# Macaron layer on one core: the outgoing tiles of the first mixture, and the routing of the second, moved into the attention loop

## Chip, cores, metric

One Trainium2 (trn2) chip, one NeuronCore. The metric is device time in microseconds of one launch, median of the runs. Engines: PE (TensorE), DVE (VectorE), ACT (ScalarE), POOL (GpSimd), and SP, which only issues DMAs here. Each engine runs its own instruction list in order; semaphores connect them.

## What is computed

The input has 2 x 2048 tokens of width 256, held in SBUF as 32 tiles of 128 tokens (`X`).

```python
x = x + 0.5 * ffn(layernorm(x))     # first mixture of experts
x = x + attn(layernorm(x))          # linear attention, 16 heads of 16
x = x + 0.5 * ffn(layernorm(x))     # second mixture, same weights
# ffn(h):  g = softmax(layer_norm(h) @ router_w.T); the two largest of 4 experts
#          hid = relu(layer_norm(h @ w1[e])) (512 wide); y_e = hid @ w2[e]
#          layer_norm(sum of the two y_e, weighted)
# attn:    Q, K, V projections; Z = cumsum over time of V K^T per head
#          Y_t = Q_t Z_t; out = Y @ Wo.T + bo
```

## The kernel before

The tokens of a mixture go in two groups G of 16 tiles (G = 0, 1 in the first mixture, 2, 3 in the second). **Routing** a group: normalise each tile (`quad_norm`, `quad_rstd`, `quad_factors`, four tiles a quad; `row` and `row_low` make an fp16 high and low part in `hrow`), transpose it (`row_T` on PE, copied by ACT), multiply by the router weights (`router`), choose experts for eight tiles, an octet (`logits`, `exps`, `choose`, `prefix`, `place`), and `scatter` each tile with two indirect DMAs from POOL's queue into the DRAM buffer `slots_in`, sorted by expert. `tables`, `positions` and `gates` then say which expert each block of 256 slots has and where each token's two results lie.

A **pair** is one block of 256 slots; a group has 19, a mixture 38. SP loads a pair (`load_slots`: two DMA transposes and one plain load, five pairs ahead), PE does `grams` (variances of the hidden layer), `layer1` and `layer2`, ACT and DVE the relu in two fp16 parts, POOL the standard deviations (`pair_std`), and SP stores the results in `slots_out` (`store_slots`). Routing group G + 1 runs beside the pairs of G, and the **outgoing tiles** of G beside the pairs of G + 1: POOL gathers a token tile's two results (`gather`, two indirect DMAs), ACT weights the first (`first_weighted`), DVE adds the second and takes statistics (`token_sum`), POOL the reciprocal root (`token_rstd`), DVE updates `X` (`token_out`). The outgoing tiles of the last group of a mixture have no pairs beside them: they run alone after the loop, and so does the routing of G = 2 (`route`), after attention.

**Attention** waits for all of X (`wait_ge(c_x, NT)` on every engine), does a prologue (POOL clears `qx`; scales, transposed weights, first block of Q, K, V), then 32 chunks of 128 tokens in blocks of four. Within a block's four chunks (t = 0 to 3) PE also does the next block's transposes, Q and K (t = 1) and V (t = 2). Per chunk: `scores` (four groups of heads), DVE masks them (`mask_scores`), ACT and POOL split them in a high part and a low part (`score_high`, `score_low`), PE `outputs` and `keys_values`, DVE `mask_kv`, POOL `add_state`, then PE `y_T` and `project` and DVE `update_x`. SP copies the queries apart by head for the scores (`expand`, eight DMAs per half block).

```python
    POOL, chunk c: score_low(c+1, 0..2); add_state(c)
    DVE,  chunk c: mask_scores(c+1, 0..1); update_x(c-1); mask_scores(c+1, 2..3); last_score_low(c+1); mask_kv(c)
    PE,   chunk c: scores(c+1), with y_T(c-1), project(c-1) between; outputs(c); keys_values(c)
```

## Time and profile before

| | us |
|---|---|
| median of 3 runs (1186.03 to 1187.82) | 1186.77 |
| the profiled execution | 1186.19 |
| its span, first to last instruction | 1184.3 |
| weights and routing of G = 0 | 0 to 118 |
| pairs of the first mixture | 118 to 392 |
| outgoing tiles of G = 1 | 392 to 454 |
| attention's prologue and its loop | 454 to 763 |
| routing of G = 2, alone | 763 to 844 |
| pairs of the second mixture | 844 to 1116 |
| outgoing tiles of G = 3, stores | 1116 to 1184 |

Busy over the span: PE 859.2 us (73%), DVE 773.1 (65%), POOL 634.1 (54%), ACT 528.3 (45%). The mean granted PE clock is 0.87 of full speed. The span is cut in stages that follow each other with little overlap, so shares of the whole say little: each stage is read by itself.

### The profile page before, as it was taken

What the parts mean: (1) busy time and instruction counts of PE and PEld (TensorE: products, weight loads), DVE (VectorE), ACT (ScalarE), POOL (GpSimd) and SP (SyncE); (2) the same over time, 40 slices, a digit from 0 to 9 for tenths busy, and PEclk for the clock granted to TensorE, in tenths of its full rate; (3) what the DMA queues carried; (4) which work ended last, traced back from release to release, by engine and by line L of the source; (5) the groups of instructions that cost most, each with busy time, mean ns of one, the idle gap of its engine ahead of it and who ended that gap; (6) DMA issues with size and microseconds to landing.
All of it is one profiled execution on the core that took longest, in us unless ns stands there. A gap on an engine that the chain in (4) does not pass through costs nothing.

```text
span 1184.3 us, 26374 instructions
## 1 busy us (share of the span) xinstructions
PE 859.2 (73%) x8346; PEld 677.6 (57%) x8346; DVE 773.1 (65%) x2160; ACT 528.3 (45%) x998; POOL 634.1 (54%) x707
## 2 busy tenths in 40 slices
PE   1543799989999202799999999730499989999600
PEld 1432688878888101466666666520388878888500
DVE  5567765776787366477777777643366675877355
ACT  2643466333434112467665666461266433444311
POOL 4154327533555476377778777537325462555275
PEclk9966899999999655899999999955599999999955
DMA  8052346656664320000000000003435655666332
GB/s 284 21 192 96 90 105 173 164 158 159 153 170 112 107 75 18 19 19 19 12 12 17 20 19 19 1 19 138 116 104 140 157 177 148 155 168 151 126 119 91
DMA packets 168026, 119.74 MB, mean 101 GB/s; under 512 B 95061, under 2 KB 158041, under 8 KB 167769
## 3 DMA queue, kind: packets, MB, share of 16 engines
q1 hardware_dynamic: 154626, 83.42, 26.7%
q0 software_dynamic: 12288, 33.57, 9.1%
q8 instruction: 77, 1.26, 0.5%
q10 hardware_dynamic: 984, 1.07, 0.3%
q14 instruction: 51, 0.42, 0.1%
HBM read 48.79 MB, written 45.09 MB: 79 GB/s over the span
## 4 chain that ended last, share of the span: by engine, by line
PE 54%; POOL 13%; DVE 11%; issue 10%; DMA 6%; ACT 5%; SPq 1%; ACTq 0%; POOLq 0%; DVEq 0%
POOL slots_in L503 6%; PE bank L1682 5%; PE bank L1669 5%; PE bank L1670 5%; PE bank L1671 5%; PE bank L1684 4%; PE bank L1683 4%; PE bank L1751 4%; PE bank L1752 4%; PE bank L1753 4%; DMA area<-slots_out,pos 4%; PE bank L1645 2%; PE bank L1851 2%; PE bank L1646 2%; PE bank L1532 2%
## 5 line engine op out<-in xcount | busy, mean ns | idle before, releaser
L511 POOL TENSOR_TENSOR stds<-vare,expo 128x4 f32<-128x4 f32 x76 | 80.4, 1058 | 200.0 <-DVE vare L794 196.5
L503 POOL DMA_INDIRECT slots_in<-area,spos x128 | 134.2, 1048 | 98.7 <-DVE spos L729 63.5
L1682 PE MATMUL bank<-w2h,area 128*128 x608 | 166.3, 274 | 3.2 <-DVE area L808 3.2
L1669 PE MATMUL bank<-area,w1h 128*128 128x256 f16 x608 | 168.2, 277 | 0.0
L1670 PE MATMUL bank<-area,w1h 128*128 128x256 f16 x608 | 168.2, 277 | 0.0
L1671 PE MATMUL bank<-area,w1l 128*128 128x256 f16 x608 | 168.0, 276 | 0.0
L1684 PE MATMUL bank<-w2h,area 128*128 x608 | 165.8, 273 | 0.0
L1683 PE MATMUL bank<-w2l,area 128*128 x608 | 165.8, 273 | 0.0
L527 POOL DMA_INDIRECT area<-slots_out,pos x128 | 126.0, 984 | 54.9 <-issue 30.5
L808 DVE SCALAR_TENSOR_TENSOR area<-bank,area 128x512 f16<-128x512 f32 x152 | 104.5, 688 | 76.6 <-ACT area L1271 74.1
L606 POOL TENSOR_TENSOR area<-area 128x512 f16<-128x512 f32 x96 | 119.3, 1265 | 56.1 <-ACT area L1452 56.1
L1271 ACT ACTIVATE area<-bank 128x512 f16<-128x512 f32 x152 | 90.0, 592 | 119.4 <-PE bank L1671 117.5
L1645 PE MATMUL bank<-gramh,area 128*128 x304 | 75.4, 284 | 55.6 <-DMA area<-slots_in 39.5
L1287 ACT ACTIVATE area<-area,gate 128x256 f32<-128x256 f32 x64 | 32.5, 508 | 177.2 <-DMA area<-slots_out,pos 177.2
L1279 ACT ACTIVATE area<-bank,stds 128x256 f32<-128x256 f32 x152 | 71.4, 470 | 80.3 <-PE bank L1684 80.1
L1753 PE MATMUL bank<-area 128*128 128x16 f16 (+2 forms) x704 | 101.9, 213 | 0.0
L1751 PE MATMUL bank<-area 128*128 128x16 f16 (+2 forms) x704 | 99.3, 213 | 2.4 <-POOL area L606 1.4
L1752 PE MATMUL bank<-area 128*128 128x16 f16 (+2 forms) x704 | 100.9, 212 | 0.0
L1452 ACT ACTIVATE area<-area 128x512 f16<-128x512 f32 x128 | 78.2, 627 | 43.1 <-DVE area L1157 42.4
L1157 DVE SCALAR_TENSOR_TENSOR area<-bank,causal 128x512 f32<-128x512 f32 x128 | 84.8, 685 | 16.8 <-POOL area L606 9.7
L1646 PE MATMUL bank<-graml,area 128*128 x304 | 75.4, 285 | 0.0
L780 DVE SCALAR_TENSOR_TENSOR area<-area 128x512 f32<-128x512 f16 x76 | 51.9, 683 | 35.3 <-DMA area<-slots_in 35.0
(267 smaller groups left out, 2231.4 us busy)
## 6 DMA issues: line engine op xcount, KB each, us to landing
area<-slots_in SPq DMA_DIRECT2D x76, 256.0 KB, 3.1
slots_out<-area SPq DMA_DIRECT2D x152, 128.0 KB, 3.2
X<-in_L_attn_x_dram SPq DMA_DIRECT2D x8, 512.0 KB, 8.7
slots_in<-zrow SPq DMA_DIRECT2D x16, 256.0 KB, 2.4
area<-area SPq DMA_DIRECT2D x128, 32.0 KB, 2.0
out_dram<-X SPq DMA_DIRECT2D x32, 128.0 KB, 1.8
area<-slots_in SPq DMA_TRANSPOSE x152
area<-in_L_ffn_w_dram SPq DMA_DIRECT2D x4, 512.0 KB, 11.1
```

The lines of the kernel that those rows point to most:

```text
L503: pool.indirect_dma_start(slots_in[G % 2], bass.IndirectOffsetOnAxis(spos[:, O % 2, k, j:j + 1], 0), hrow[:, t].rearrange("p c d -> p (c d ...
L527: pool.indirect_dma_start(d[:, i % R_C], None, slots_out[G % 2], bass.IndirectOffsetOnAxis(pos[:, G % 2, k, t:t + 1], 0)).then_inc(g_y[i % ...
L606: pool.tensor_tensor(shl[:, c % 2, 1, g], sm[:, g], shl[:, c % 2, 0, g], ALU.subtract).then_inc(a_sl, 1)
L1669: pe.matmul(o, w1h[c][m][:, bass.ds(e, 1), :], a[:, c], start=(c == 0), stop=False)
L1670: pe.matmul(o, w1h[c][m][:, bass.ds(e, 1), :], a[:, KC + c], start=False, stop=False)
L1671: last = pe.matmul(o, w1l[c][m][:, bass.ds(e, 1), :], a[:, c], start=False, stop=(c == KC - 1))
L1682: pe.matmul(o, Rh[:, p % 2, k, rows], w2h[k][:, bass.ds(e, 1), :], start=(k == 0), stop=False)
L1683: pe.matmul(o, Rh[:, p % 2, k, rows], w2l[k][:, bass.ds(e, 1), :], start=False, stop=False)
L1684: last = pe.matmul(o, Rl[:, p % 2, k, rows], w2h[k][:, bass.ds(e, 1), :], start=False, stop=(k == HC - 1))
L1751: pe.matmul(o, lh, rh, start=start, stop=False, **kw)
L1752: pe.matmul(o, lh, rl, start=False, stop=False, **kw)
L1753: return pe.matmul(o, ll, rh, start=False, stop=stop, **kw)
```

## The change

Everything that lay between the last pair of the first mixture and attention's loop, and between that loop and the first pair of the second, is put elsewhere:

- The outgoing tiles of G = 1 go in chunks 0 to 17 of attention: chunk c gathers tile c, weights and sums tile c - 1, and updates X with tile c - 2. They use buffers of their own (`yA1`, `yB1`, `acc1`).
- The routing of G = 2 goes in chunks 5 to 28: one row per chunk from chunk 7 on, octets chosen from chunks 16 and 24, four scatters in each of chunks 19 to 22 and 27 to 30. Its rows are transposed by DMA (`turn_row`, on SP) and no longer by PE and ACT.
- The rows of G = 2 need 32 KB per partition while attention holds its own buffers. They take the place of the second weights: `w2h` and `w2l` become one tile `w2all`, written to DRAM (`w2_kept`, 2 MB) when the first mixture begins and read back after SP's first five pair loads of the second.
- Attention's prologue goes beside the first mixture's pairs (`ahead`): weights loaded at the start, maxima at j = 14, scales at 16, transposed weights from 16, POOL's clearing of `qx` at j = 0 of the second group, the first rows at 10 to 13, the first queries ahead of the last `layer2`.
- The queries of attention are expanded per chunk (`expand(c)`, eight DMAs of half the size for each of 32 chunks, not for each of 16 halves), and `hTh`, `hTl` and `qx` have other shapes.

```diff
+    w2_kept = nc.dram_tensor("w2_kept", (P, 2 * HC * E * D), F16).ap()
...
-            def expand(n):
-                wait(sp, a_qp, n + 1)
-                for part in range(2):
-                    cols = slice(part * BT // 2, (part + 1) * BT // 2)
-                    wait(sp, a_s, NG * TB * (n - 1) + NG * 2 * (part + 1))
-                    for j in range(HPC):
-                        rows = slice(j * HD, (j + 1) * HD)
-                        sp.dma_start(qx[rows, j, :, :, cols], qp[rows, :, :, cols]).then_inc(a_qx[part], 16)
+            def expand(c):
+                wait(sp, a_qp, c // TB + 1)
+                wait(sp, a_s, NG * (c - 1))
+                cols = slice(c % TB * P, (c % TB + 1) * P)
+                for j in range(HPC):
+                    rows = slice(j * HD, (j + 1) * HD)
+                    sp.dma_start(qx[rows, c % 2, j], qp[rows, :, :, cols]).then_inc(a_qx[c % 2], 16)
+            def turn_row(i):
+                sp.wait_ge(r_hl, i + 1)
+                wait(sp, r_L, i - 1)
+                sp.dma_start_transpose(turned_of(i), rows_of(i).rearrange("p c d -> p (c d)")
+                                       ).then_inc(l_tT[i % 2], 16)
+            def attention():
+                sp.wait_ge(a_zero, 1)
+                expand(0)
+                expand(1)
+                for c in range(NT):
+                    if c + 2 < NT:
+                        expand(c + 2)
+                    if row_in(c) is not None:
+                        turn_row(row_in(c))
...
+                else:
+                    sp.wait_ge(m_w2, 16)
+                    sp.dma_start(w2flat, w2_kept).then_inc(m_w2, 16)
...
             def attention():                        # POOL
-                pool.wait_ge(c_x, NT)
...
                         add_state(c)
+                        if c < GT:
+                            gather(GT + c)
+                        if 1 <= c <= GT:
+                            token_rstd(GT + c - 1)
+                        if quad_in(c) is not None:
+                            quad_rstd(quad_in(c))
+                        if quad_in(c - 1) is not None:
+                            quad_again(quad_in(c - 1))
+                        for i in moves_in(c):
+                            scatter(i)
...
                             mask_scores(c + 1, 1)   # DVE
+                        if 2 <= c <= GT + 1:
+                            token_out(GT + c - 2)
                         if c > 0:
+                            wait(dve, a_wo, c)
+                            if octet_in(c, 0) is not None:
+                                logits(octet_in(c, 0))
+                            if octet_in(c, 2) is not None:
+                                place(octet_in(c, 2))
                             update_x(c - 1)
...
+                        if 1 <= c <= GT:
+                            token_sum(GT + c - 1)
+                        if row_in(c) is not None:
+                            row_low(row_in(c))
+                        if quad_in(c) is not None:
+                            quad_norm(quad_in(c))
+                        if octet_in(c, 1) is not None:
+                            choose(octet_in(c, 1))
...
+                        if 1 <= c <= GT:            # ACT
+                            first_weighted(GT + c - 1)
+                        if row_in(c) is not None:
+                            row(row_in(c))
...
-                    route(G)                        # PE, second mixture
+                    pe.wait_ge(a_x, NT)
```

How it moves the lists. POOL inside attention's loop, from the start of a block to the third chunk (L606 and L703 are `score_low`, L612 and L709 `add_state`, L596 and L693 `add_bias`). Before:

```order
L606 TENSOR_TENSOR area<-area 128x512 x3
L612 TENSOR_TENSOR area<-area 128x256
L606 TENSOR_TENSOR area<-area 128x512 x3
L596 TENSOR_TENSOR X<-X,boB 128x1024
L612 TENSOR_TENSOR area<-area 128x256
L606 TENSOR_TENSOR area<-area 128x512
```

And now, for one of the blocks of chunks 4 to 15:

```order
L703 TENSOR_TENSOR area<-area 128x512 x3
L709 TENSOR_TENSOR area<-area 128x256
L610 DMA area<-slots_out,pos 128x256 x2
L600 TENSOR_TENSOR ars<-ave,nhalf 128x1
L703 TENSOR_TENSOR area<-area 128x512 x3
L693 TENSOR_TENSOR X<-X,boB 128x1024
L709 TENSOR_TENSOR area<-area 128x256
L610 DMA area<-slots_out,pos 128x256 x2
L600 TENSOR_TENSOR ars<-ave,nhalf 128x1
L569 TENSOR_TENSOR xrs<-xve,nhalf 128x4
L703 TENSOR_TENSOR area<-area 128x512
```

Each chunk has two gathers (L610) and a reciprocal root (L600) behind its `add_state`, and two chunks of a block one more root of the routing (L569, L574).

DVE inside the loop, from the second chunk of a block (t = 1) to the third. Before, from the end of the chunk (L1127 is `query_low`, L1157 `mask_scores`, L1170 `update_x`):

```order
L1175 SCALAR_TENSOR_TENSOR area<-bank,sameh 128x256
L1127 TENSOR_TENSOR area<-area 128x2x512
L1157 SCALAR_TENSOR_TENSOR area<-bank,causal 128x512 x2
L1170 TENSOR_TENSOR X<-bank,X 128x256
L1157 SCALAR_TENSOR_TENSOR area<-bank,causal 128x512 x2
```

Now (L1242 is `query_low`, L1272 `mask_scores`, L1285 `update_x`):

```order
L1242 TENSOR_TENSOR area<-area 128x2x512
L926 SCALAR_TENSOR_TENSOR area<-area,gate 128x256
L929 BN_STATS ast<-area 128x6
L931 BN_AGGR amv<-ast 128x2
L932 TENSOR_SCALAR ave<-amv 128x1
L777 TENSOR_TENSOR w2all<-area,w2all 128x256
L758 BN_STATS xst<-X 128x6 x4
L761 BN_AGGR xmv<-xst 128x2 x4
L763 TENSOR_SCALAR xve<-xmv 128x4
L1272 SCALAR_TENSOR_TENSOR area<-bank,causal 128x512 x2
L937 SCALAR_TENSOR_TENSOR area<-area,amv,ong 128x256
L941 SCALAR_TENSOR_TENSOR X<-area,ars,X 128x256
```

Between `query_low` and the next chunk's masks stand `token_sum` (L926 to L932), `row_low` (L777) and `quad_norm` (L758 to L763), and `token_out` (L937, L941) stands between the second and the third mask.

SP in the first mixture, behind the fifth pair load. Now:

```order
L458 DMA area<-slots_in 128x2x512
L478 DMA area<-in_L_attn_Wq_dram 128x2x256
L478 DMA area<-in_L_attn_Wk_dram 128x2x256
L478 DMA area<-in_L_attn_Wv_dram 128x2x256
L478 DMA area<-in_L_attn_Wo_dram 128x2x256
L481 DMA w_kept<-w2all 128x8192
L452 TENSOR_LOAD rtab
```

The weights' loads (1 MB) and the copy of `w2all` (2 MB) stand ahead of the sixth pair's load; before, L435 loaded the weights after the last store.

## Rows read from the trace of the kernel before

**Rows 1.** Stages: stretch, length, busy PE, PEld, DVE, ACT, POOL; clock, DMA share, GB/s.

```profile
393.00:454.00 61.00, 0.00 (x0) 0.00 (x0) 33.34 (x95) 8.12 (x16) 41.59 (x48) 0.53 0.30 88
454.00:494.00 40.00, 23.03 (x99) 13.46 (x100) 19.61 (x38) 13.75 (x21) 15.11 (x17) 0.66 0.05 13
494.00:762.00 268.00, 253.02 (x2862) 175.85 (x2861) 197.51 (x305) 169.93 (x296) 199.31 (x226) 0.99 0.07 16
762.00:847.00 85.00, 18.02 (x202) 14.02 (x201) 32.97 (x152) 24.55 (x51) 42.13 (x42) 0.52 0.22 78
```

**Rows 2.** Timeline of PE, around the last layer2 and attention's second chunk.

```profile
391.86 0.27 PE L1684 MATMUL bank<-w2h,area 128*128 x1
...
493.13 0.39 PE L1751 MATMUL bank<-area 128*128 128x512 f16 x1 [0.52 <-DVE area L1157]
493.35 0.38 PE L1752 MATMUL bank<-area 128*128 128x512 f16 x1
```

**Rows 3.** PE: eight f32 transposes; its wait at the first group's end; SP's expand DMAs.

```profile
610.23 1.04 PE L1737 MATMUL bank<-identf,h 128*128 128x128 f32 x8
...
PE bank L1645 <- DMA area<-slots_in: 2.2, 1, 2.2
...
L429 SPq DMA_DIRECT2D area<-area x128: 585/595/1571, 482.3 to 733.7; - x128
```

**Rows 4.** The chain of waits in attention's prologue: maxima, and the scales' first and last step.

```profile
456.15 2.05 DVE mx L1099 x3
...
462.40 0.17 DVE mxa L846
...
464.69 0.27 DVE bvB L1115
```

**Rows 5.** One block of attention by chunk (t = 0 to 3), columns as in Rows 1.

```profile
601.20:608.00 6.80, 6.08 (x77) 4.09 (x77) 5.17 (x12) 4.26 (x9) 5.66 (x15) 1.00 0.01 4
608.00:620.20 12.20, 12.20 (x109) 7.61 (x110) 7.70 (x12) 9.44 (x16) 9.36 (x8) 1.00 0.01 2
620.20:629.40 9.20, 9.20 (x109) 7.32 (x108) 6.92 (x12) 5.02 (x10) 6.62 (x5) 1.00 0.20 48
629.40:636.00 6.60, 5.65 (x76) 3.91 (x76) 6.11 (x8) 3.77 (x7) 4.42 (x4) 1.00 0.07 16
```

**Rows 6.** Groups by line: gathers (393 to 454), scatters and `row_low` (762 to 847).

```profile
L527 POOL DMA_INDIRECT area<-slots_out,pos x32 | 31.1, 972 | 18.7 <-DMA slots_out<-area 11.0 <-issue 7.7
...
L503 POOL DMA_INDIRECT slots_in<-area,spos x32 | 31.9, 997 | 25.6 <-DVE spos L729 16.2 <-issue 9.4
...
L675 DVE TENSOR_TENSOR area<-h,area 128x256 f16<-128x256 f32 x16 | 6.6, 423 | 14.3 <-ACT area L1247 14.3
```

**Rows 7.** Two DVE lines and one of POOL: ns shortest/median/longest, first and last start.

```profile
L1164 DVE TENSOR_TENSOR area<-area x32: 691/1140/1643, 495.6 to 755.8; 128x512 f16<-128x512 f32 x32
...
L1133 DVE TENSOR_TENSOR area<-bank,area x16: 678/686/692, 484.1 to 729.3; 128x512 f16<-128x512 f32 x16
...
L606 POOL TENSOR_TENSOR area<-area x96: 1147/1157/2146, 493.8 to 755.2; 128x512 f16<-128x512 f32 x96
```

**Rows 8.** From attention's end to the second mixture's first layer2: chain, then timelines.

```profile
763.26 1.41 DVE xst L655 x4
...
832.68 0.96 POOL L503 DMA_INDIRECT slots_in<-area,spos  x1 [0.30 <-issue]
...
854.65 0.53 SPq L396 DMA_DIRECT2D area<-slots_in  x1
...
859.66 0.27 PE L1682 MATMUL bank<-w2h,area 128*128 x1
```

**Rows 9.** Four loads of 256 KB on SP's queue: timeline, then the last one's landing.

```profile
393.09 0.39 SPq L435 DMA_DIRECT2D area<-in_L_attn_Wq_dram  x1
...
394.58 0.47 SPq L435 DMA_DIRECT2D area<-in_L_attn_Wo_dram  x1
...
area<-in_L_attn_Wo_dram SPq DMA_DIRECT2D x1, 256.0 KB, 4.3
```

More of the change, by code:

```diff
@@ L285, in macaron_kernel @@
             "kv_added"))
-        a_qx = [sem(f"a_q_expanded{half}") for half in range(2)]
+        a_qx = [sem(f"a_q_expanded{b}") for b in range(2)]
+        l_tT = [sem(f"rows_T_{b}") for b in range(2)]
+        m_w2 = sem("w2_kept_and_back")
         dve_done = sem("dve_done")
@@ L344, in token_bank, with octet_in, row_in, router_in @@
             return bank[3] if i < GT else bank[4]
+        ROW_AT = 7
+        LOGITS_IN = [ROW_AT + 2 + TO * (o + 1) - 1 for o in range(GO)]
+        def octet_in(c, d):
+            return GO * 2 + LOGITS_IN.index(c - d) if c - d in LOGITS_IN else None
+        def row_in(c):
+            return 2 * GT + c - ROW_AT if 0 <= c - ROW_AT < GT else None
+        def router_in(c):
+            return row_in(c - 2)
+        def moves_in(c):
+            for o, at in enumerate(LOGITS_IN):
+                if at + 3 <= c < at + 3 + TO // 2:
+                    t = 2 * GT + TO * o + 2 * (c - at - 3)
+                    return t, t + 1
+            return ()
+        def quad_in(c):
+            return 2 * GQ + (c - 5) // TB if c % TB == 1 and 0 <= (c - 5) // TB < GQ else None
         @block.sync
@@ L1392, in mixture, with ahead, queries_ahead @@
                         row_T(i0 + GT + t)
+                    if f == 0:
+                        ahead(g - G, j)
+                if f == 0:
+                    queries_ahead()
                 for k in range(2):
                     scale_out(p0 + NP - 1, k)
-                for t in range(GT):
-                    first_weighted(i0 + GT + t)
+                if f == 1:
+                    for t in range(GT):
+                        first_weighted(i0 + GT + t)
+            def ahead(second, j):
+                if not second and j in (17, 18):
+                    weight_high(j - 17)
+                if second and j in (0, 1):
+                    weight_high(2 + j)
+                if second and j in (10, 11):
+                    h_rows(0, range(2 * (j - 10), 2 * (j - 9)))
+                if second and j == 12:
+                    hT_high(0)
+            def queries_ahead():
+                for o in range(GO):
+                    act.wait_ge(sc_h[o], 32 * TO * 2)
+                qk_copy(0, 0, qf[:, 0])
+                query_high(0)
             def h_rows(n, tiles):
@@ L1429, in query_high @@
             def query_high(n):
-                for part in range(2):
-                    wait(act, a_qx[part], NX * n)
+                for b in range(2):
+                    wait(act, a_qx[b], NX * 2 * n)
                 wait(act, a_qf, 4 * n + 2)
@@ L1549, in row_T @@
                 pe.wait_ge(r_hl, i + 1)
-                wait(pe, r_hT, i)
+                wait(pe, r_hT, turned(i))
                 if i == 0:
@@ L1728, in mixture, with ahead @@
                         row_T(i1 + t)
+                    if f == 0:
+                        ahead(g - G, j)
+                if f == 0:
+                    queries_keys(0, 0)
                 for k in range(2):
                     layer2(p0 + NP - 1, k, e[p0 + NP - 1])
+            def ahead(second, j):
+                if not second and j == 14:
+                    maxima_T(3)
+                if not second and j == 15:
+                    maxima_all(3)
+                if not second and j in (16, 17, 18):
+                    weight_T(j - 16)
+                if second and j == 0:
+                    weight_T(3)
+                if second and j == 11:
+                    pe.wait_ge(a_wl, 3)
+                    pe.wait_ge(a_wh, 4)
+                    rows_out_T(0)
             def rows_out_T(n):
```

285 lines of the change are left out of this document (161 added, 124 removed).

## The prediction

> **What bounds the kernel now.** I read the windows by stage first. Two stretches leave PE nearly idle: the outgoing tiles and the prologue (393 to 494, PE busy 23 of 101 us), and the routing (762 to 847, PE 18 of 85) [rows 1]. In the 268 us of attention's loop PE is busy 253, so the loop is PE's; but POOL has 199 and DVE 198 there, so each has only some 70 us free. The idle stretches are bought with that room. Then I read one block of the loop by chunk: 34.8 us, of which POOL works 26.1 and DVE 25.9; PE fills the chunks t = 1 and t = 2 wholly, while in t = 0 and t = 3 DVE has 1.6 and 0.5 us free and POOL 1.1 and 2.2 [rows 5]. So new work in t = 0 and t = 3 lengthens the loop at once.
>
> The sum is made against the profiled execution, 1186.2 us (span 1184.3, 1.9 around it); the median lies 0.6 above it.
>
> **A, the prologue's work beside the pairs: +12.** PE gets 24 f32 transposes at 1.04 / 8 = 0.13 us [rows 3], 3.1 us, and 12 matmuls of 512 columns at 0.22 us, the distance of two neighbours [rows 2], 2.6 us. PE is full in these pairs, so all 5.7 count. It also waits in order for others: for DVE's maxima 2.05 us, for the scales from 462.40 to 464.96, 2.6 us [rows 4], and for ACT's first rows some 1.7. That is 6.3, less the 2.2 us that PE waits for the second group's slots anyway [rows 3], since the maxima and scales fall just before that: +4. The weights and the 2 MB copy stand ahead of the sixth pair's load on SP; five pairs are loaded by then and cover them, so 0 to 5 us, I take 2. POOL's clearing (one 7 us instruction) falls where it has no gather; cover gone, it would delay one pair by under 5. A is 6 to 20.
>
> **B, what stood between: -87.8.** From the last `layer2` (ends 392.13) to the scores of chunk 1 (493.13) are 101.0 us [rows 2]. What is left: 12 matmuls for the keys (2.6 us), eight transposes (1.0), 24 matmuls of 256 columns for the values (at half of 0.22, 2.6), twelve for chunk 0's scores (2.6) and the copies between, some 11 us in sequence; and SP, after its last two stores (about 1.6 us), issues 16 expand DMAs at 0.595 each [rows 3], 9.5, and 2 to land: 13.2. SP is the later: 101.0 - 13.2 = 87.8, between 80 and 90.
>
> **C, attention's loop: +80.** Step by step.
> POOL: 16 outgoing tiles cost what the tail cost, 41.6 us [rows 1], plus 0.3 of issue time for each of 32 gathers [rows 6]: 51, or 3.2 per chunk. Routing costs 42.1 + 9.4 = 51.5 in the same way [rows 1, 6], of which scatters are four per chunk in eight chunks, 5.1 us each time. Together 102 against 69 free: **at least +33**, even if POOL never waits.
> DVE: the tail's 33.3 us are 2.1 per tile [rows 1]; the routing's 33.0 [rows 1] are 0.42 per row [rows 6], per quad 1.4 of statistics [rows 8] and some small steps, about 2.7 with them, and the rest, some 15, for the two octets and the tables. Together 66 against 70 free.
> DVE is also slower beside POOL: its subtraction with both inputs in SBUF (L1164) has a median of 1140 ns, and the same shape with one input in PSUM (L1133) 686 [rows 7]. The 0.45 us between them I add to each of the new two-input steps (three per tile, one per row).
> By block, then: block 0 (chunks 0 to 3), no routing yet, +6. Blocks 2 and 3: DVE 25.9 + 4 x 2.1 + 4 x 0.4 + 2.7 + 16 x 0.45 = 45.8, so +11, and 1 for waits: +12 each; POOL 26.1 + 12.8 + 2.0 = 40.9 is close behind. Block 1, with one row, +10. Block 4 (last tile, quad, first octet, first scatters) +9. Block 5: POOL 26.1 + 15.3 = 41.4, +8, since chunk t = 1 takes one set of scatters free. Block 6 (octet, tables) +9. Block 7: POOL 13.8 of 22.4 us and 15.3 more: +9 with its waits. Sum 75, and 5 for the longer round between engines, since `token_out` waits for POOL between two masks and holds the scores behind it. C is 33 at the least; I take 60 to 105 as its own range.
> Hidden: ACT gets 8.1 us (tiles) and less than 24.6 (routing, whose copies of transposed rows are gone) into 98 free. PE had 18 us for the routing at a clock of 0.52 of full speed, transposes included [rows 1]; without them and at full clock under 8 are left, where PE now waits longer than that. SP gets 128 more DMAs at 0.6 us, 4.8 per chunk in all, and 16 transposes; a chunk is 6.6 at the shortest, so its queue keeps up, unless `turn_row`, which waits for DVE's row and stands ahead of the next `expand`, makes it late; that is a rival.
>
> **D, routing taken out: -70.** Before, attention ended at 763.2 and the last scatter's issue at 833.64 [rows 8]. Now the last scatter is issued in chunk 30, within a microsecond of attention's end, and from there the second mixture starts as before: 70.4, less 0.5.
>
> **E, the second weights come late: +7.** SP issued the fifth pair's last load at 855.2, 21.5 us after the last scatter [rows 8]; the 2 MB are behind it. 1 MB took from 393.09 to 394.58 + 4.3 = 398.9, 5.8 us [rows 9], so 2 MB take 11.6: landed at 866.8 on the old scale, and `layer2` was at 859.66 [rows 8]. 0 to 15. What is late next is nothing: the sixth pair's slots land two pairs before use.
>
> Sum: 12 - 87.8 + 80 - 70 + 7 = -58.8, so **1127 us**, faster by 5%. The end of the kernel (68 us) is untouched.
>
> **A rule weighed.** The row first: L606 on POOL, which also reads SBUF, has a median of 1157 ns and a longest of 2146, DVE's L1164 of 691 to 1643 [rows 7]: they do hold each other up. The Trainium skill, "SBUF — State Buffer", section "Who interferes with whom", says that a DVE instruction with two SBUF inputs and a GpSimd instruction that reads SBUF exclude each other, and that the later one waits for the whole of the other. By that, this change puts more of both kinds side by side. The trace agrees for DVE's median; for POOL only the longest shows it. By the rule in full the loop would be the third rival; by the rows it is the 0.45 us above.
>
> **Rivals.**
> *POOL's floor.* The engines shift against each other by up to a chunk, waits vanish and C falls to 33 to 60, say 45: 1092 us. For it: POOL's 69 free us would then be used whole. Against: PE's t = 1 chunk holds everybody for 12.2 us, and DVE is nearly as full as POOL.
> *The round is longer.* `expand` waits behind `turn_row`, which waits for ACT's row, behind ACT's wait for the gather. In 16 chunks SP then issues 1.2 + 4.8 + 2 us late into a 6.6 us chunk: about 1.5 us each, 24; with some 10 more of waits C is 105 to 135: at 115, 1162 us. For it: SP's list is in order. Against: there is a chunk of slack.
> *Slower: DVE and POOL lock each other.* Each of the 96 L606 takes its longest, 2146 for 1157 ns [rows 7], +0.99 us: 95 us more on the engine that sets the pace, so C is 175 and the time 1222. It decides from C = 139 on, that is 1.8 us per chunk above my sum. Against: only a few of the 96 are long today, with DVE 74% busy.
> That the parts do not overlap is no rival: the lists above show them within the loop. Were the weights' return much slower (27 us), it is 15 us and inside the range.
>
> **Numbers.** My forecast (1108 to 1153) 0.61; POOL's floor (1080 to 1108) 0.20; longer round (1153 to 1186) 0.15; lock 0.04. Leaving out a tenth on each side, the range is 1093 to 1162. A difference under 0.2% (2.4 us) could not be told from none. Faster 0.96, same 0.01, slower 0.03.
>
> **What would show it.** Chunk 1's scores 10 to 15 us after the last `layer2`; blocks 2 and 3 of the loop at 44 to 49 us with POOL and DVE busy over 85%, PE under 75%; the loop as a whole 340 to 360 us; PE waiting 5 to 10 us for the DMA of `w2all` at the second mixture's first `layer2`. I am wrong if a block stays under 41 or goes over 52 us, or if PE waits in the first mixture for more than 12 us above before.

## The result, and the profile after

| | before | after |
|---|---|---|
| median, us (5 runs each, side by side) | 1186.95 | 1192.67 |
| span of the profiled execution | 1184.3 | 1191.8 |

The ratio is 1.0032, 95% interval 1.0017 to 1.0048: **slower by 0.3%**, where 1127 us was forecast. I cut the profiled execution as the prediction did. The windows by stage (columns as in [rows 1]) of the changed kernel, then the one stage of the kernel before that [rows 1] lacks, then its loop and the changed one from the first `update_x` to the last:

```profile
118.00:417.71 299.71, 272.48 (x2490) 226.87 (x2491) 211.42 (x670) 134.27 (x269) 133.61 (x141) 0.95 0.55 140
417.71:430.30 12.59, 9.07 (x58) 5.28 (x55) 5.46 (x8) 5.30 (x8) 2.12 (x1) 1.00 0.15 42
430.30:836.00 405.70, 304.51 (x2982) 198.39 (x2982) 309.18 (x545) 192.28 (x347) 279.49 (x314) 0.86 0.15 39
836.00:864.90 28.90, 13.61 (x100) 9.20 (x100) 17.50 (x73) 7.28 (x14) 6.76 (x7) 0.72 0.70 172
442.00:835.60 393.60, 295.06 (x2899) 192.85 (x2897) 300.11 (x528) 184.47 (x332) 269.25 (x297) 0.86 0.15 40
```

```profile
118.00:392.13 274.13, 261.08 (x2450) 219.79 (x2450) 193.99 (x640) 126.17 (x255) 124.84 (x126) 0.97 0.55 140
505.00:762.90 257.90, 245.38 (x2785) 171.11 (x2783) 189.53 (x291) 162.76 (x282) 189.24 (x209) 1.00 0.07 16
```

The terms, by the same boundaries (end of the last `layer2`, first scores of chunk 1, end of attention, first `layer2` of the second mixture):

| term | forecast | measured, us |
|---|---|---|
| A, prologue beside the pairs | +12 | 417.71 - 392.13 = +25.6 |
| B, what stood between | -87.8 | 12.6 - 101.0 = -88.4 |
| C, attention's loop | +80 | 405.7 - 270.1 = **+135.6** |
| D and E, routing out, weights late | -63 | 29.1 - 96.4 = -67.3 |
| after that | 0 | +2.1 |

They add up to 7.6, and the spans differ by 7.5. The idle stretches went about as forecast (156 us, 151 forecast); the loop and the first mixture took 161 back.

These are terms of one execution. The first mixture is the same code in the changed kernel and in twelve of the kernels below (e1 to e7, e9 to e11, e14, e16), and its last `layer2` begins between 408.92 us (e6) and 417.44 (the changed kernel, the latest of all), with a median of 413.3. So A is +17 to +26, and about +21 is the usual value.

No engine is full in the loop: of 393.6 us DVE is busy 300, PE 295, POOL 269. Windows of four chunks, from `update_x` to `update_x`; the prediction had blocks 2 and 3, which the third of them and the next (54.6 us) lie over, at 44 to 49 us:

```profile
442.00:497.40 55.40, 41.84 (x433) 27.94 (x431) 44.94 (x65) 24.78 (x44) 42.18 (x48) 0.88 0.13 35
497.40:552.90 55.50, 41.47 (x374) 26.67 (x374) 42.74 (x80) 26.00 (x47) 38.49 (x44) 0.82 0.13 34
552.90:610.80 57.90, 41.50 (x392) 26.42 (x392) 43.48 (x83) 28.02 (x51) 38.96 (x44) 0.84 0.16 37
```

All of these windows are above 52 us, which the prediction had named as a sign of being wrong. DVE's 43 us of work in a block are near what the prediction's sum gives (45.8); it expected them to fill the block, and they fill 75 to 81% of it. PE's waits in the loop (waiting line, releaser, sum, times, longest), and SP's longest:

```profile
PE bank L1930 <- DMA area<-area: 24.0, 8, 4.7
PE bank L1930 <- DVE area L1248: 21.4, 8, 4.0
PE bank L1930 <- DVE X L1285: 17.3, 10, 4.5
PE bank L1930 <- DVE hTl L1205: 8.4, 4, 2.6
...
SPq L507 <- DVE w2all L777: 118.4, 16, 16.6
```

L1930 is the first line of the helper that makes most of PE's products; L1248 is `ktok_low`, L1285 `update_x`, L1205 the low part of the transposed rows, L507 `turn_row`. Before, PE stood idle for 15 us in the whole loop (268.0 - 253.0). And DVE's lines there, with the mean of one in ns: L1279, `last_score_low` (L1164 in [rows 7], mean 1154), L941, the last step of `token_out` (485 where it ran alone), and L773, a step of `quad_factors` (170 there):

```profile
L1279 DVE TENSOR_TENSOR area<-area 128x512 f16<-128x512 f32 x32 | 53.8, 1682 | 7.7 <-ACT area L1605 7.7
L941 DVE SCALAR_TENSOR_TENSOR X<-area,ars,X 128x256 f32<-128x256 f32 x16 | 23.9, 1495 | 7.7 <-issue 6.7 <-DVE area L937 0.5
...
L773 DVE TENSOR_SCALAR r2t<-r2t 128x4 f32<-128x4 f32 x4 | 3.2, 802 | 0.1
```

One case, as the timelines of DVE and POOL show it (start, duration):

```profile
574.39 1.07 DVE L770 SCALAR_TENSOR_TENSOR xnr<-xmv,xrs 128x4 f32<-128x4 f32 x1
575.38 0.15 DVE L772 TENSOR_TENSOR r2t<-r2t,xrs 128x4 f32<-128x4 f32 x1
575.57 1.01 DVE L773 TENSOR_SCALAR r2t<-r2t 128x4 f32<-128x4 f32 x1
576.49 1.28 DVE L1248 TENSOR_TENSOR area<-bank,area 128x512 f16<-128x512 f32 x2
...
574.30 2.26 POOL L703 TENSOR_TENSOR area<-area 128x512 f16<-128x512 f32 x2
```

Two of `quad_factors`' steps of 128x4 end, within 0.1 us, with POOL's two subtractions; they stand ahead of `ktok_low` in DVE's list, and PE waits for that one, 3.98 us, until 577.23. A DVE step can be held by several POOL instructions in a row, too. Here `last_score_low`, 0.68 us at its shortest, takes 6.21, and ends 0.55 us after the fourth POOL instruction that had followed without a gap:

```profile
445.60 6.21 DVE L1279 TENSOR_TENSOR area<-area 128x512 f16<-128x512 f32 x1
...
445.58 3.37 POOL L703 TENSOR_TENSOR area<-area 128x512 f16<-128x512 f32 x3
448.92 2.34 POOL L693 TENSOR_TENSOR X<-X,boB 128x1024 f32<-128x1024 f32 x1
```

Two theories follow. **The round**: a step added ahead of what PE waits for lengthens each chunk, whatever share of DVE is free. **The lock**: DVE is held by POOL, more than I had priced, wherever the step stands.

### The profile page after: what moved, and what is told of

It is laid out like the page before. It is cut to its first block and busy times, and to the rows that moved or that the text cites. A ratio compares the mean times of both kernels' runs of the same rounds, so it can differ in the third digit from the quotient of the medians.

```text
span 1191.8 us, 26435 instructions
## 1 busy us (share of the span) xinstructions
PE 895.7 (75%) x8282; PEld 688.3 (58%) x8282; DVE 824.3 (69%) x2172; ACT 514.9 (43%) x982; POOL 629.9 (53%) x707
## 5 line engine op out<-in xcount | busy, mean ns | idle before, releaser
L1845 PE MATMUL bank<-w2all,area 128*128 x608 | 166.6, 274 | 7.0 <-DMA w2all<-w_kept 4.8
L1846 PE MATMUL bank<-w2all,area 128*128 x608 | 166.3, 274 | 0.0
L1847 PE MATMUL bank<-w2all,area 128*128 x608 | 166.3, 273 | 0.0
L610 POOL DMA_INDIRECT area<-slots_out,pos x128 | 126.3, 987 | 45.9 <-issue 29.4
L586 POOL DMA_INDIRECT slots_in<-area,spos x96 | 103.9, 1082 | 74.2 <-DVE spos L831 48.5
L703 POOL TENSOR_TENSOR area<-area 128x512 f16<-128x512 f32 x96 | 118.3, 1253 | 46.6 <-ACT area L1605 46.5
L1930 PE MATMUL bank<-area 128*128 128x16 f16 (+2 forms) x704 | 107.5, 221 | 43.3 <-DMA area<-area 24.0
L1932 PE MATMUL bank<-area 128*128 128x16 f16 (+2 forms) x704 | 107.8, 220 | 0.0
L1931 PE MATMUL bank<-area 128*128 128x16 f16 (+2 forms) x704 | 107.5, 220 | 0.0
L1806 PE MATMUL bank<-gramh,area 128*128 x304 | 77.3, 289 | 30.6 <-DMA area<-slots_in 12.1
L1930 PEld LDWEIGHTS bank<-area 128*128 128x128 f16 x704 | 60.0, 99 | 53.8 <-DMA area<-area 25.7
L1272 DVE SCALAR_TENSOR_TENSOR area<-bank,causal 128x512 f32<-128x512 f32 x128 | 82.5, 681 | 10.7 <-PE bank L1932 8.0
## 6 DMA issues: line engine op xcount, KB each, us to landing
area<-in_L_ffn_w_dram SPq DMA_DIRECT2D x4, 512.0 KB, 12.8
```

Of the source, the lines that this page charges most:

```text
L586: pool.indirect_dma_start(slots_in[G % 2], bass.IndirectOffsetOnAxis(spos[:, O % 2, k, j:j + 1], 0), rows_of(i).rearrange("p c d -> p (c d ...
L610: pool.indirect_dma_start(d[:, i % R_C], None, slots_out[G % 2], bass.IndirectOffsetOnAxis(pos[:, G % 2, k, t:t + 1], 0)).then_inc(g_y[i % ...
L703: pool.tensor_tensor(shl[:, c % 2, 1, g], sm[:, g], shl[:, c % 2, 0, g], ALU.subtract).then_inc(a_sl, 1)
L1845: pe.matmul(o, Rh[:, p % 2, k, rows], w2h[k][:, bass.ds(e, 1), :], start=(k == 0), stop=False)
L1846: pe.matmul(o, Rh[:, p % 2, k, rows], w2l[k][:, bass.ds(e, 1), :], start=False, stop=False)
L1847: last = pe.matmul(o, Rl[:, p % 2, k, rows], w2h[k][:, bass.ds(e, 1), :], start=False, stop=(k == HC - 1))
```

## Experiments

Ratios are to the kernel before, run beside each. "Loop" is from the first `update_x` to the last, in one profiled execution: 257.9 us before, 393.6 changed. What a kernel gains over the changed one is given by medians. By the ratios it is 1 to 3 us less: 6 (e1), 25 (e5), 13 (e6), 40 (e7), 20 (e14), 10 (e16). The loop alone, free of the first mixture's variation, gives 5, 18, 13, 38, 17 and 10.

### Which part costs: e1 to e4

e1 moves the transposing DMA behind the next expanding ones:

```diff
-                    if row_in(c) is not None:
-                        turn_row(row_in(c))
+                    if row_in(c - 1) is not None:
+                        turn_row(row_in(c - 1))
```

> The change with one edit: SP issues the DMA transpose of a routing row one chunk later, behind the next chunk's eight expand DMAs and not ahead of them. Theory 'round' (the loop is long because its steps follow each other across engines, and SP's turn_row, which waits for DVE's row_low at the end of a chunk, holds the expand DMAs that PE's scores need): PE's wait for the expand DMAs in the loop falls from 24 us to under 5 and the kernel is 15 to 35 us faster, near 1165. Theory 'lock' (DVE and POOL hold each other up and the length is theirs): the wait moves to another name and the time stays within 5 us of 1192.

Measured: 1183.53 us, ratio 0.9981 (0.9959 to 1.0004), 9 us under the changed kernel (6 by the ratios), loop 388.7. That is neither theory's time. PE's wait for the DMA fell from 24.0 us to 1.4, as the round theory said, but waits for ACT and DVE rose in its place, as the lock theory said.

e2 runs the outgoing tiles of G = 1 alone, after the first mixture, and leaves the routing in the loop; e3 does the reverse; e4 leaves both out of the loop, so that only the early prologue, the weights in DRAM and the queries expanded per chunk are new. The calls leave the loop and come back, unchanged, outside it, as in e2:

```diff
-                        if c < GT:
-                            gather(GT + c)
-                        if 1 <= c <= GT:
-                            token_rstd(GT + c - 1)
...
-                if f == 1:
+                if True:
                     for t in range(GT + 1):
```

> The change with the outgoing tiles taken out of attention's chunks and run alone behind the first mixture, as before; the routing stays beside attention. The tail comes back with 58 us. Theory 'lock': the tiles bring 48 of the two-input DVE steps and 32 gathers, so most of the loop's growth of 149 us goes with them, over 90, and the kernel is near 1155. Theory 'round' with SP as its centre: chunks 7 to 22 keep their long round through turn_row, the loop loses only 50 to 60 and the kernel is near 1190 to 1200.

> The change with the routing of G = 2 taken out of attention's chunks and run alone behind it (rows still turned by DMA), the outgoing tiles stay beside attention. Routing alone comes back with 60 to 75 us. Theory 'round': chunks 7 to 31 get most of their length back, the loop loses 80 to 100, kernel near 1165 to 1180. Theory 'lock': the loop loses 45 to 60, since the tiles' steps stay, kernel near 1205.

> The change with both taken out of attention: what is left of it is the prologue beside the pairs, the weights kept in DRAM and the expand per chunk. Both theories: the loop is back at 270 to 280 us, so the kernel is near 1186 - 40 (prologue) + 15 (its work beside the pairs) + 7 (weights) = 1160 to 1175. If it is over 1185, the expand per chunk or the prologue's part costs what the loop seemed to cost.

| | us | ratio, interval | loop |
|---|---|---|---|
| e2, routing in the loop | 1205.27 | 1.0175, 1.0137 to 1.0214 | 349.2 (+91.3) |
| e3, tiles in the loop | 1189.81 | 1.0044, 1.0024 to 1.0063 | 324.9 (+67.0) |
| e4, neither | 1190.71 | 1.0047, 1.0027 to 1.0067 | 257.9 (0) |

e4's loop is as long as before (257.9 us, PE busy 245.38 in both): 256 smaller DMAs cost the loop nothing. Tiles alone cost 67 and routing alone 91, together 136: the two costs overlap. No theory had the times of e2 and e3: e2's loop lost 44 us (over 90 or 50 to 60 were expected), e3's 69 (80 to 100 or 45 to 60). e4, expected at 1160 to 1175, came to 1190.71, and by its stages the early prologue is why: the first mixture is 23.0 us longer (15 expected), from there to the first `update_x` it is only 24.5 shorter (88.4 for 112.9; 40 expected), and what follows the loop is 7.5 longer (7 expected). In e3, tile steps stretch a block (492.0 to 543.0) from 34.8 us to 51, with DVE busy 37.6 of it, POOL 36.1 and PE 39.3.

### Place in the queue: e5 to e7

e5 moves `token_out` from ahead of `update_x`, between the masks, to the chunk's end. e6 leaves only the reads out of PSUM of `logits` and `place` there, and moves the rest and `quad_factors` to the end. e7 does both, and e1's move. No step is removed.

```diff
-                        if 2 <= c <= GT + 1:
-                            token_out(GT + c - 2)
                         if c > 0:
...
+                        if 2 <= c <= GT + 1:
+                            token_out(GT + c - 2)
                         if 1 <= c <= GT:
                             token_sum(GT + c - 1)
+                        if octet_in(c, 0) is not None:
+                            logits_rest(octet_in(c, 0))
...
+                        if quad_in(c - 1) is not None:
+                            quad_factors(quad_in(c - 1))
```

> The changed kernel, with the outgoing step (token_out) moved on VectorE from ahead of update_x to the end of the chunk, just before token_sum; nothing is removed. The round theory (what stands ahead of update_x lengthens each chunk, since TensorE waits for update_x and its transposes): the 1.5 us mean of 16 such steps and their place beside the gathers leave the round; the loop from first to last update_x comes down from 393.6 us by 16 x 1.5 to 2.4 = 24 to 38 us, and the time to 1155 to 1170. The lock theory (VectorE is held by GpSimd's two-operand instructions wherever the step stands): the step costs the same at its new place and the queue behind it moves on as late; the loop changes by less than 8 us, the time stays at 1184 to 1196, and the mean of the step stays near 1.5 us.

> The changed kernel, with the routing's small steps moved on VectorE to the end of the chunk: of logits and place only the read out of PSUM stays ahead of update_x, and quad_factors no longer stands ahead of ktok_low. Round theory: in the chunks that hold them the 4 to 8 us between the masks and ktok_low go down; loop shorter by 15 to 30 us, time 1160 to 1178. Lock theory: each of these small steps is held for 1 to 2 us wherever it stands, so the loop changes by less than 8 us and the time stays at 1184 to 1196.

> Both moves of the two runs before, and the transposing DMA of the routing rows one chunk later, behind the next expanding DMAs. Round theory: the gains add up to 45 to 75 us: 1117 to 1148 us, and the loop 320 to 350 us. Lock theory: the gain is that of the late DMA alone (about 9 us): 1176 to 1186 us.

| | us | ratio, interval | loop |
|---|---|---|---|
| e5 | 1166.58 | 0.9821, 0.9800 to 0.9843 | 375.3 |
| e6 | 1177.31 | 0.9924, 0.9908 to 0.9941 | 380.8 |
| e7 | 1150.36 | 0.9696, 0.9672 to 0.9719 | 355.7 |

The same work in another order is 42 us faster, and the parts nearly add up: 26 (e5), 15 (e6) and 9 (e1) against 42; in the loop 18, 13 and 5 against 38. That is the round in each of the three, not the lock theory's less than 8 us (about 9 in e7), though the loops gained less than expected (18 for 24 to 38, 13 for 15 to 30, 38 for 44 to 74) and e7 came 2 us above its range. e5's lines show that the lock is not apart from it:

```profile
L1279 DVE TENSOR_TENSOR area<-area 128x512 f16<-128x512 f32 x32 | 56.6, 1768 | 7.7 <-ACT area L1605 7.7
...
L941 DVE SCALAR_TENSOR_TENSOR X<-area,ars,X 128x256 f32<-128x256 f32 x16 | 11.4, 711 | 0.6
```

At its new place `token_out`'s step is held far less (711 ns, not 1495; one at 548.23 us, beside two gathers of POOL, takes 0.48 us); `last_score_low`, which did not move, is held as before. In e7 the loop is

```profile
437.50:793.20 355.70, 289.42 (x2899) 191.66 (x2896) 287.53 (x528) 185.41 (x332) 271.58 (x297) 0.88 0.17 44
```

with its first block at 45.4 us, DVE busy 42.1 of them: there DVE comes near to setting the pace, as the prediction had it.

### The first mixture: e8

```diff
-                if not second and j == 14:
+                if not second and j == 12:
                     attention_maxima()
-                if not second and j == 15:
+                if not second and j == 14:
                     max_row(3)
-                if not second and j == 16:
+                if not second and j == 15:
                     attention_scales()
```

(and TensorE's two steps one pair earlier, the first rows' turn one pair later.)

> The kernel of e7_all_late, with the prologue's steps beside the first mixture's pairs spaced out: on VectorE the maxima of the attention weights two pairs earlier, their row and the scales one pair earlier; on TensorE their two steps one pair earlier; the turn of the first block's rows (TensorE, ScalarE, VectorE) one pair later. Theory: term A came to 25.6 us and not 12 because TensorE stood 5.4, 4.7 and 2.7 us for exactly these three steps, placed in the same pair as the step that feeds them. Then these 12.8 us go, and the time is 1137 to 1145 against 1150. Rival: the stretch is longer because VectorE has too much to do there; then the waits come back at other lines and the time stays at 1148 to 1153.

In the changed kernel PE's waits of the first mixture are these (the fourth and fifth of them are the turn of the first rows and the first weight):

```profile
PE bank L1806 <- DVE var L891: 8.6, 2, 8.1
PE bank L1699 <- DVE mx L1212: 5.4, 1, 5.4
PE bank L1806 <- issue: 4.9, 9, 1.2
PE bank L1914 <- ACT h L1553: 4.7, 1, 4.7
PE bank L1924 <- DVE bvB L1230: 2.7, 1, 2.7
```

Measured: 1140.69 us, ratio 0.9607 (0.9591 to 0.9624), 9.7 below e7, with those three waits gone and the one for `mxd` grown from 0.7 to 3.3 us. The theory holds: a step and the one that feeds it stood in one pair.

### Three ways to mend the loop further: e9, e11, e13

e9 gives `last_score_low` to POOL. e11 moves the prefix matmul, `place` and the scatters one chunk later, and leaves out the loop's `positions(2)` and `gates(2)`. e13 (on e12, below) puts `mask_kv` ahead of `last_score_low`. Of e9's edit, the line that changes engine:

```diff
-                dve.tensor_tensor(shl[:, c % 2, 1, NG - 1], sm[:, NG - 1], shl[:, c % 2, 0, NG - 1],
+                pool.tensor_tensor(shl[:, c % 2, 1, NG - 1], sm[:, NG - 1], shl[:, c % 2, 0, NG - 1],
```

> The kernel of e7_all_late, with the low part of the fourth score group (last_score_low) on GpSimd instead of VectorE: VectorE loses 32 steps, 66.0 us of busy time, GpSimd gains 32 of about 1.2 us = 38 us. Lock theory (VectorE's busy time is in good part time in which it is held by GpSimd, and it sets the block): VectorE falls from 42 to 34 us of a block of 49, and the loop gets 10 to 30 us shorter: 1120 to 1140. Floor theory (GpSimd, at 39 of 49 us, is as near to its own end as VectorE): GpSimd comes to 44 us a block, PE waits for its low parts instead, and the loop is unchanged or up to 15 us longer: 1150 to 1165.

> The kernel of e7_all_late, with the prefix matmul, place and the scatters one chunk later (so that TensorE does not stand for choose, 5.7 us in two waits), and without the loop's positions(2) and gates(2), which the second mixture computes again. Theory: 5.7 us of TensorE's wait and about 3 us of VectorE in chunk 28 leave: 1141 to 1147. Rival: VectorE sets the chunk wherever the wait shows, and only the left-out steps count: 1147 to 1151.

> The kernel of e12_steps_before_query, with mask_kv ahead of last_score_low in each chunk. Theory: TensorE's projection waited 10.4 us for mask_kv, which stood behind a step that GpSimd holds for 1 to 4 us; that wait goes and the time falls by a further 5 to 12 us. Rival: mask_kv has to wait for TensorE's keys_values, and last_score_low behind it gets late for the next outputs: no gain, or up to 8 us slower.

Measured: e9 1157.28 us (ratio 0.9751, 0.9705 to 0.9796), e11 1151.31 (0.9706, 0.9687 to 0.9725), e13 1143.64 (0.9632, 0.9594 to 0.9670). None gains in time. In e9 DVE's busy time falls by 41 us, to 246.0 in this window, and the loop grows by 7, to 363.1:

```profile
437.50:800.00 362.50, 287.57 (x2899) 189.50 (x2898) 246.00 (x498) 185.69 (x333) 303.10 (x328) 0.87 0.17 43
```

POOL's busy time grew by 32 us, `query_low` went from a mean of 1319 to 2578 ns, PE waits 12.1 us for POOL (as the floor theory said, whose range the time is in) and 17.6 us for `update_x` (5.6 in e7). In e11 the loop is 5.6 us shorter than e7's (350.1), just what the wait for `choose` was, but what stands after the loop is 4.3 us longer (359.6 for 355.3): the steps left out are done there. In e13, where the rival's up to 8 us came about, the held step's mean falls from 1994 to 1723 ns, the loop is 4.7 us longer than e12's, and the wait for `update_x` grows from 8.5 to 13.9 us.

### What the routing is worth: e10

e10 is e3 with e5's move.

> The kernel of e3_routing_alone (only the outgoing tiles in the loop, the second routing after attention), with token_out at the chunk's end. If the gain of e5 (26 us) belongs to the tiles' place alone, it comes again here: 1189.8 - 26 = 1164, within 5. It then also prices the routing in the loop: kernel e7 (1150) less this one. If the gain needed the routing beside it, this stays above 1175.

Measured: 1167.88 us, ratio 0.9825 (0.9800 to 0.9851), 22 below e3 (26 by the ratios), within the 5 us that were allowed: the gain of e5 comes again. Its loop:

```profile
440.70:738.90 298.20, 263.06 (x2785) 176.32 (x2783) 246.72 (x388) 169.09 (x298) 233.28 (x257) 0.95 0.11 28
```

So the outgoing tiles, well placed, cost the loop 40 us (67 in e3). The routing on top of them costs 57.5 (e7) and saves about 72 after it: 17.5 us by the medians (1167.88 - 1150.36), of which some 3 are the first mixture's variation. In the changed kernel's order it cost 68.6 (e3's loop to the changed one): nearly all of the 70.5 that it saved.

### The steps where DVE waits: e12

In the second chunk of a block DVE stood for ACT's split of the queries (3.6 us in block 5) with the tile's steps behind the wait:

```diff
-                        if t == 1 and not last:
-                            query_low(n + 1)
...
                         if octet_in(c, 1) is not None:
                             choose(octet_in(c, 1))
+                        if t == 1 and not last:
+                            query_low(n + 1)
```

> The kernel of e8_prologue_early, with the tile and routing steps of the second chunk of each block put ahead of query_low, where VectorE stood 3.6 us for ScalarE's split of the queries in block 5. Theory: the steps fill that wait, 2 to 3.5 us in each of some 6 blocks: 12 to 20 us of the loop, time 1121 to 1130. Rival: query_low then comes too late for the next block's scores, or the steps meet GpSimd's two-operand instructions there and are held; gain below 5 us, 1136 to 1142.

Measured: 1138.05 us, ratio 0.9589 (0.9561 to 0.9617), 2.6 under e8 with overlapping intervals, loop 352.1 (e8 356.9): the rival. It is the lowest of all that ran, with e15 and e8 indistinguishable beside it.

### The lock alone: e14

```diff
-                pool.tensor_tensor(shl[:, c % 2, 1, g], sm[:, g], shl[:, c % 2, 0, g], ALU.subtract).then_inc(a_sl, 1)
+                pool.tensor_scalar(shl[:, c % 2, 1, g], sm[:, g], 0.0, None, ALU.mult).then_inc(a_sl, 1)
```

> The changed kernel itself, with GpSimd's low parts of the scores (96 steps, mean 1253 ns) made by an instruction that reads one array instead of two (the score times 0): the low parts of three score groups are left out of the result. Lock theory (VectorE's holds, 47 us more than before, come from GpSimd's steps that read two arrays, and they are what lengthened the loop): VectorE's last_score_low goes from 1682 ns back to about 690, token_out's step from 1495 to about 500, and the time falls by 35 to 60 us, below 1158. Round theory (the place of the steps in VectorE's queue costs, the holds are a smaller part): the holds shrink all the same, but the time falls by the part of them that stands ahead of update_x and the masks only, 10 to 30 us: 1163 to 1183. If GpSimd's one-input step takes as long and holds VectorE as much, nothing changes and two inputs are not what holds.

Measured: 1171.19 us, ratio 0.9863 (0.9824 to 0.9903), 21.5 below the changed kernel, though POOL's step itself became longer. DVE's busy time in the loop fell by 44 us (300.1 to 256.3), the loop by 17 (376.8): most of the held time lay beside the path. One-line views of POOL's and of DVE's step (ns shortest/median/longest), the changed kernel, then e14:

```profile
L703 POOL TENSOR_TENSOR area<-area x96: 1142/1157/2137, 430.8 to 826.7; 128x512 f16<-128x512 f32 x96
...
L1279 DVE TENSOR_TENSOR area<-area x32: 676/1154/6211, 432.5 to 824.9; 128x512 f16<-128x512 f32 x32
```

```profile
L703 POOL TENSOR_SCALAR area<-area x96: 1477/1492/2397, 425.3 to 805.2; 128x512 f16<-128x512 f32 x96
...
L1279 DVE TENSOR_TENSOR area<-area x32: 680/692/3052, 427.0 to 798.2; 128x512 f16<-128x512 f32 x32
```

The long holds that are left lie beside a step that still reads two arrays: e14's longest are three beside `add_bias` (L693). Beside the new L703 `token_out`'s step takes 0.71 to 0.89 us, where it takes 0.48 alone, and L1279 0.68 to 1.09:

```profile
538.20 0.77 DVE L941 SCALAR_TENSOR_TENSOR X<-area,ars,X 128x256 f32<-128x256 f32 x1 [2.94 <-issue]
542.29 3.05 DVE L1279 TENSOR_TENSOR area<-area 128x512 f16<-128x512 f32 x1
...
538.06 4.42 POOL L703 TENSOR_SCALAR area<-area 128x512 f16<-128x512 f32 x3
542.45 2.33 POOL L693 TENSOR_TENSOR X<-X,boB 128x1024 f32<-128x1024 f32 x1
```

So the lock is real, and taking most of it away is worth 17 to 21 us in the changed kernel, with POOL's slower step (0.3 us each) already in the sum: inside what the round theory gave it and half of what the lock theory did. It overlaps with the places. The edit changed both the operation and the number of arrays, so these runs can't tell which of the two matters; and it was not tried on the mended order (e7, e12), where `last_score_low` is held even longer (a mean of 2061 ns in e7).

### TensorE's clock: e15 and e16

Neither theory had this. After the wait of 3.98 us, the matmuls of the values come 0.21 us apart, where they came 0.11 apart before; windows of 4 us on PE alone (length, busy, clock, DMA, GB/s), then two of these matmuls, and the same two in the kernel before:

```profile
572.90:576.90 4.00, 0.34 (x6) 0.86 0.06 13
576.90:580.90 4.00, 3.67 (x18) 0.50 0.00 0
```

```profile
577.84 0.42 PE L1930 MATMUL bank<-wTh,hTh 128*128 128x256 f16 x1
578.05 0.42 PE L1931 MATMUL bank<-wTl,hTh 128*128 128x256 f16 x1
...
625.00 0.27 PE L1751 MATMUL bank<-wTh,hTh 128*128 128x256 f16 x1
625.11 0.27 PE L1752 MATMUL bank<-wTl,hTh 128*128 128x256 f16 x1
```

The clock stands at its lower level, 1.2 of 2.4 GHz. I took windows of 1 us over the loop and multiplied PE's busy time in each by its granted clock: 245.4 us before, 252.5 changed, 251.4 in e7. PE's work hardly grew; its busy time did (245.4 to 295.1). So of C's 135.7 (393.6 - 257.9), 86.0 are pauses of PE, 42.6 lower clock and 7.1 work. Whether the 42.6 lie on the path is what e15 (on e12) and e16 (on the changed kernel) ask, with matmuls that nobody reads in PE's pauses:

```diff
+            def warm(o, times):
+                for _ in range(times):
+                    pe.matmul(o[:, :], ident16[:, :], w1h[0][0][:, 0:4, :], start=True, stop=True)
...
+                        if t == 2 and not last:
+                            wait(pe, a_sm, NG * (c + 1) + 1)
+                            warm(bank[0], 14)
```

> The kernel of e12_steps_before_query, with filler matmuls (128x128 by 512 columns, 0.22 us each, their result read by nobody, into score banks whose masks are done): 9 before the wait for ktok_low in the third chunk of a block, 5 before each projection. Clock theory (TensorE's pauses of 1 to 4 us are followed by stretches at 0.50 granted clock, 86 of the loop's 352 us not at full clock, which lengthen its work by 30 us): the loop's mean clock rises from 0.89 to over 0.95, of the 30 us most go, less what the fillers delay where there was no wait: time 1118 to 1132. Rival (TensorE is not on the round's path where its clock is low, or the fillers cost as much as they save): 1134 to 1145.

> The changed kernel itself with such fillers: 14 before the wait for ktok_low, 6 before each chunk's first score (the wait for the expanded queries), 5 before each projection; nothing else is moved. Clock theory: of the 43 us by which the lower clock lengthens TensorE's work in the loop (busy 295.1 us, 252.5 if each stretch is weighed by its clock) 20 to 35 come off the time: 1158 to 1173. Rival: VectorE's queue and its holds set the round and TensorE's slow stretches lie beside them: less than 8 us, 1185 to 1197.

Measured: e16 1179.80 us, ratio 0.9947 (0.9928 to 0.9966), 13 under the changed kernel; e15 1138.45, ratio 0.9588 (0.9558 to 0.9618), no gain over e12. e16's loop:

```profile
436.90:820.10 383.20, 347.84 (x3321) 220.41 (x3318) 295.39 (x528) 184.84 (x332) 269.85 (x297) 0.97 0.16 41
```

The clock is back (0.97, from 0.86; the same product leaves 10.2 us lost, from 42.6), and it gave 10 us of the loop (10 by the ratios as well). e16 also puts PE's wait for the masks ahead of that for the expanded queries. So most of the slow stretches lay beside the path: between the two ranges for e16, the rival for e15. What the fillers themselves cost was not measured apart.

## Why the prediction was wrong

**A, +12, was mis-sized: +25.6 in this execution, about +21 as a rule.** The condition named for being wrong (PE waiting over 12 us more in the first mixture) came true here, though not by much: PE's idle time there went from 13.1 to 27.2 us (24.3 in e7, 22.0 in e6, with the same code). Maxima, first rows and scales were priced at 6.3 together by the length of each step alone. They cost 5.4 + 4.7 + 2.7 = 12.8, since in the list of DVE or ACT the pair's own work stood ahead of the first two; the scales cost what they were priced at. The wait for the first rows is also what varies most: 4.7 here, 1.7 in e6. The 2.2 us of wait for slots that I set off did vanish, but waits for issue rose from 2.4 to 4.9. PE's busy time rose by 11.4, not 5.7. e8 takes back 9.7, and with its order A is +11.6 (e12's last `layer2` ends at 403.7).

**B, D and E were right**: 88.4 for 87.8, and D and E together 67.3 for 63; the weights' copy landed in 8.4 us (11.6 forecast), and PE waited 4.8 for it (5 to 10 forecast):

```profile
L1845 PE MATMUL bank<-w2all,area 128*128 x608 | 166.6, 274 | 7.0 <-DMA w2all<-w_kept 4.8
```

**C, +80, is the step that failed: +135.6.** Its sum of work was nearly right and its conversion into time was not. DVE's busy time rose by 112 us, holds included (66 and 29 for the two-input steps were forecast), POOL's by 80 (102 with some 19 of issue time in it). The prediction then took the excess of the fuller engine's busy time over the block, and 5 us for the round. What the runs show instead, in overlapping amounts that are not to be added:

- *The order inside the chunk, 42 us by the medians, 38 of the loop* (e7, with e1's move in it). The prediction named this very point ("`token_out` waits for POOL between two masks and holds the scores behind it") and gave it 5 us.
- *The hold of DVE by POOL, 17 to 21 us* (e14). I priced 0.45 us per new two-input step. `token_out`'s step was held by 1495 - 485 = 1.0 us, steps of 128x4 by up to 0.9 us, and `last_score_low`, an old step, went from a mean of 1154 to 1682 ns; no term had the old steps in it.
- *The transposing DMA ahead of the expanding ones, 5 to 9 us* (e1). That was my rival "the round is longer", which put 24 on it.
- *The lower clock after pauses, 10 to 13 us* (e16). It was in no term: in the loop before, the clock was 1.00 throughout, and I took it as given.

With order and prologue mended (e12) the kernel stands at 1138, 11 above the forecast and inside its range, and its loop at +94. With better places, then, term C is 14 us from its estimate; in the order given, 56. Where those 14 come from is not shown: lock and clock are still in that loop, and only the clock was tried there (e15, no gain).

**The rivals.** POOL's floor (C 33 to 60) was reached by no kernel with both parts in the loop: the shortest such loop, e11's, is 350.1 us, +92. The lock was to decide from C = 139, by lengthening POOL's 96 steps to 2146 ns. C came to 136, but not so: POOL's median is 1157 ns as before, its mean 1253 (1265 before). The change held DVE more, and POOL's subtraction no more than before. The Trainium skill, "SBUF — State Buffer", section "Who interferes with whom", says that the two exclude each other and that the later one waits for the whole of the other. That DVE waits for the whole, the case at 574.39 agrees with; the one at 445.60 waits for four in a row. That POOL would pay as DVE does, these runs don't bear out. By its words any GpSimd instruction that reads SBUF holds a two-input step; in e14 one that reads a single array held it by 0.4 us at most, not for its whole 1.5.

## What to carry over

Room on an engine is no room in a round: before moving work beside a loop, look at what stands behind it in the same engine's list and who waits for that, and put it at the chunk's end, behind what feeds the next engine. Keep VectorE's steps with two SBUF inputs away from GpSimd's two-input ones, and count the old steps that a new neighbour will hold. Here the loop in which TensorE hardly paused (12.5 of 257.9 us) ran at full clock, and with 98.5 us of pauses its work got longer too.

## What the runs showed of the hardware

- VectorE's `tensor_scalar` on 128x4 (L773) took a mean of 802 ns in the loop of the changed kernel (three of four 1.01 us, beside a GpSimd subtraction), 170 in e14, where GpSimd's step reads one array, and 170 in e7, where the step stands at the chunk's end: even a tiny step with one input was held.
- GpSimd's 128x512 step took 1157 ns (median) as a subtraction of two arrays and 1492 as a product of one array and a constant: fewer operands were slower.
- A VectorE step can wait for a whole run of GpSimd instructions: 6.21 us for 0.68 at 445.60, beside four that followed without a gap.
- Many of TensorE's pauses in the loop were followed by stretches at a granted clock of 0.50, where the loop before ran at 1.00. The pause's length alone did not decide: in e12, after pauses of 2.56 us before the same matmuls, the next 3 us had a clock of 0.55 at 542.65 and 1.00 at 591.45. Filling the pauses raised the mean from 0.86 to 0.97 and gave 10 to 13 us, under a third of the 42.6 that the clock had added to TensorE's busy time; in e15 it gave nothing.
